# The second image pair with pixel parity alternating by row, and the half-height tap products of both pairs as quarter tiles

## Time and profile before

| | |
|---|---|
| median of 3 runs | 2612.29 us (2609.6 to 2612.97) |
| profiled execution | 2612.23 us, its span 2610.4 us |
| mean granted PE clock | 0.989 |
| instructions | 117000, of them 46070 matmuls |
| DMA | 155.07 MB, mean 59 GB/s |
| input loaded, first block | 0 to 143 us |
| sweeps 0 to 3 | 143 to 1249 us |
| sweeps 4 to 7 | 1261 to 2366 us |
| last block | to 2610 us |

### The profile page before, as it was taken

The page is one execution under the profiler, slowest core; times in us unless marked ns, Lnnn a source line. Parts: engine busy times, 40 slices in busy tenths (PEclk is TensorE's granted clock), DMA queues, the critical chain, the costliest instruction groups (busy, mean ns, idle before and its releaser), DMA issues. The chain is left out here.

```text
span 2610.4 us, 117000 instructions
## 1 busy us (share of the span) xinstructions
PE 2509.8 (96%) x46070; PEld 2417.0 (93%) x46070; DVE 1813.5 (69%) x5782; ACT 1236.6 (47%) x2705; POOL 352.7 (14%) x547
## 2 busy tenths in 40 slices
PE   1999999999999999999899999999999999998998
PEld 1389999999999999999899999999999999997885
DVE  7866666666666666677666666666666666777986
ACT  0866664222233333377666642222333333675877
POOL 1620000000000000066000000000000000653545
PEclk9999999999999999999999999999999999998999
DMA  7810001222450000087600012223600000430006
GB/s 270 219 45 0 0 0 36 61 60 60 91 54 0 0 4 1 0 258 161 190 8 0 0 29 60 60 60 88 66 0 0 0 0 0 129 97 2 4 4 258
DMA packets 323834, 155.07 MB, mean 59 GB/s; under 512 B 155169, under 2 KB 319650, under 8 KB 319650
## 3 DMA queue, kind: packets, MB, share of 16 engines
q1 hardware_dynamic: 321600, 153.41, 22.9%
q10 hardware_dynamic: 2146, 0.53, 0.1%
HBM read 70.00 MB, written 50.33 MB: 46 GB/s over the span
## 5 line engine op out<-in xcount | busy, mean ns | idle before, releaser
L870 PE MATMUL banks<-x_row,w_taps 128*64 128x124 f32 (+2 forms) x40640 | 2200.4, 270 | 5.4 <-DVE x_row L1114 3.1
L870 PEld LDWEIGHTS banks<-x_row,w_taps 128*64 128x64 f32 x40640 | 2198.8, 135 | 7.1 <-issue 6.1
L1123 DVE SCALAR_TENSOR_TENSOR x_row<-banks,sweep_nbias,biased_row 128x128 f32<-128x128 f32 x2032 | 712.9, 351 | 717.1 <-PE banks L870 695.1
L666 ACT ACTIVATE biased_row<-state,sweep_bias 128x256 f32 (+1 forms) x762 | 512.2, 673 | 1038.9 <-DVE state L1126 605.7
L662 ACT ACTIVATE biased_row<-state,aff,gn_a 128x64 f32 (+1 forms) x1016 | 364.2, 429 | 184.4 <-DVE state L1132 184.4
L1126 DVE SCALAR_TENSOR_TENSOR state<-banks,sweep_nbias,biased_row 128x128 f32 (+1 forms) x1016 | 443.0, 436 | 0.0
L550 POOL TENSOR_TENSOR state<-state,stripe_a 128x256 f32<-128x256 f32 x96 | 66.9, 733 | 1982.3 <-DVE state L1126 1962.0
L1132 DVE SCALAR_TENSOR_TENSOR state<-banks,sweep_nbias,biased_row 128x64 f32 (+1 forms) x1016 | 236.9, 275 | 0.1
L1132 DVE SCALAR_TENSOR_TENSOR turn_ring<-banks,sweep_nbias,biased_row 128x64 f32<-128x64 f32 x1016 | 236.7, 274 | 0.0
L843 PE MATMUL banks<-res,ffn_w 64*64 64x512 f32 x512 | 112.3, 597 | 6.1 <-ACT res L599 5.2
L832 PE MATMUL banks<-state,ffn_s 64*64 64x512 f32 x512 | 106.8, 598 | 0.2 <-DVE ffn_s L1285 0.2
(11 more groups left out here) (138 smaller groups left out, 903.3 us busy)
## 6 DMA issues: line engine op xcount, KB each, us to landing
state<-turn_ring SPq DMA_DIRECT2D x512, 64.0 KB, 1.9
resid<-state SPq DMA_DIRECT2D x94, 256.0 KB, 3.6
state<-x_in SPq DMA_DIRECT2D x16, 1024.0 KB, 20.7
stripe_a<-resid SPq DMA_DIRECT2D x32, 512.0 KB, 5.3
stripe_b<-resid SPq DMA_DIRECT2D x32, 512.0 KB, 5.4
out_y<-state SPq DMA_DIRECT2D x16, 1024.0 KB, 4.1
res<-resid SPq DMA_DIRECT2D x32, 256.0 KB, 7.3
resid<-state SPq DMA_DIRECT2D x16, 512.0 KB, 6.7
```

The source lines that it names most:

```text
L666: nc.scalar.activation(as_cells(n, biased_row[:, k, :, :]), cells(n, slice(0, B), i, k, g), ACT.Identity, bias=sweep_bias[:, n:n + 1]).the ...
L870: last = nc.tensor.matmul(out_ps[blk, :, lo:hi], w_taps[:, n % 2, s, blk], x_row[c][src][:, :, s + lo:s + hi], start=at == 0, stop=at == T ...
L1123: nc.vector.scalar_tensor_tensor(x_row[c][par][:, :, 2:2 + HALF], ps, nb, br, ALU.max, ALU.add).then_inc(row_ready[c], 1)
```

## The change

The second image pair gets another layout: pixel parity sits on partition half q in even rows and on the other half in odd rows. In the sweeps down and up its conv therefore reads from the halves crosswise in turn, step by step. The weights are kept as ten 64-column slots (nine taps and one unused) per partition half, in two versions, one with the halves exchanged; the unused slots are never read. A conv now consists of four whole products for each output parity (shifts 2, 1, 3, and shift 0 for one parity with shift 4 for the other) and of the two remaining half-height ones, `single_taps`: 64x64 tiles, the diagonal quarters of the array for pair 0, the others for pair 1. Pair 0 has them at its end and pair 1 at its start, so that the four are neighbours in PE's program, and PE's wait for pair 1's row moves ahead of pair 0's last whole product.

With that go:
- block 0's result is kept as `resid_rows` in DRAM in its own layout, and the odd rows of images 2 and 3 are read back with the halves exchanged (`swap_back`), two chunks behind; `turn_residual` then makes `resid` from it by 64 DMAs inside DRAM, on SyncE's queue before sweep 1's turning; ScalarE waits for the swapped chunks in sweep 0;
- in the turned sweeps only images 0 and 1 go through `turn_ring` and DMAs. The second pair needs no move across partitions; GpSimd stores its rows with two copies a step (`store_turned`), and VectorE writes only `x_row` for it, after `row_stored[1]` of two steps before;
- between the blocks `cross` is four DMAs of half the size in place of two;
- after sweep 7 all odd rows are stored to DRAM and, once the kv products are done, those of images 2 and 3 are read back exchanged, 64 DMAs on SyncE's queue ahead of the output's stores; PE waits for them in the last feed-forward net before image 2 of each chunk, and ScalarE and GpSimd wait for the store;
- `gram_sb` and `o1_a` now lie in the weight buffer; `gram_sb` is zeroed after sweep 6; the memset of `w_taps` goes.

The core of the diff (lines that only declare semaphores, or waits of the same form, left out):

```diff
-        turn_ring = sb("turn_ring", [P, 2, 2, 2, B, WH])
-        w_taps = sb("w_taps", [P, 2, TAPS2, P])
+        turn_ring = sb("turn_ring", [P, 2, 2, 2, 2, WH])
+        w_taps = sb("w_taps", [P, 2, 2, 2 * TAPS2, C])
...
+            def swap_back(j, odd, done):
+                view = resid_rows.rearrange("p (hp r g b w) -> p hp r g b w", r=2, g=2, b=B, w=WH)
+                hp = slice(j * CR // 2, (j + 1) * CR // 2)
+                for q in range(2):
+                    into, frm = slice(q * C, (q + 1) * C), slice((1 - q) * C, (2 - q) * C)
+                    for g in range(2):
+                        sp.dma_start(state_b[into, hp, odd, g, 2:4, :].rearrange("c hp b w -> c hp (b w)"),
+                                     view[frm, hp, odd, g, 2:4, :].rearrange("c hp b w -> c hp (b w)")).then_inc(done, 16)
+            for j in range(CHUNKS + SWAP_LAG):
+                if j < CHUNKS:
+                    sp.wait_ge(ffn_added, j * B + B)
+                    sp.dma_start(resid_rows[:, j * CR * ROW:(j + 1) * CR * ROW],
+                                 state[:, j * CR:(j + 1) * CR, :, :, :].rearrange("p r g b w -> p (r g b w)")).then_inc(rows_kept[j], 16)
+                if j >= SWAP_LAG:
+                    sp.wait_ge(rows_kept[j - SWAP_LAG], 16)
...
+                    swap_back(j - SWAP_LAG, 1, rows_swapped[j - SWAP_LAG])
...
+                for q in range(2):
                     for r in range(2):
+                        block(slice(0, 2), q, r, r, q)
+                        block(slice(2, 4), q, r, q ^ r, q)
+            for part in range(TURN_PARTS):
+                turn_residual(slice(part * PAIRS // TURN_PARTS, (part + 1) * PAIRS // TURN_PARTS))
...
+            sp.wait_ge(last_rows_kept, 32)
+            sp.wait_ge(kv_done, KV_TILES)
+            for j in range(CHUNKS):
+                swap_back(j, 1, rows_swapped[j])
...
+                def store(i, k):
+                    pool.wait_ge(row_ready[1], i * 2 + (hbase(n) + k))
+                    row = x_row[1][slot(n, k)]
+                    for blk, at in ((low, row_of(True, i, k)), (high, row_of(True, i, 1 - k))):
+                        if k == 0 and blk == high:
+                            pool.wait_ge(biased_row_ready, i * 2 + (row_count(n) + 1))
+                        last = nc.gpsimd.tensor_copy(state[blk, at, :, 2:4, :],
+                                                     by_halves(row[blk, :, 2:2 + HALF]))
+                    last.then_inc(row_stored[1], 1)
...
-                pe.wait_ge(row_ready[c], hcount)
-                for at, s in enumerate(TAP_ORDER):
-                    lo, hi = max(0, EDGE - s), min(HALF, HALF + EDGE - s)
-                    for q in range(2):
-                        blk = slice(q * C, (q + 1) * C)
-                        last = nc.tensor.matmul(out_ps[blk, :, lo:hi], w_taps[:, n % 2, s, blk], x_row[c][src][:, :, s + lo:s + hi],
-                                                start=at == 0, stop=at == TAPS2 - 1)
+                halves_of = [slice(q * C, (q + 1) * C) for q in range(2)]
+                weights = w_taps[:, n % 2, 1 if c and not par else 0]
+                crossed = c and par
+                def product(inner, r, s, start, stop):
+                    lo, hi = (0, HALF) if start else (max(0, EDGE - s), min(HALF, HALF + EDGE - s))
+                    return nc.tensor.matmul(out_ps[halves_of[1 - r if crossed else r], :, lo:hi], weights[inner, 2 * s + 1 - r, :],
+                                            x_row[c][src][inner, :, s + lo:s + hi], start=start, stop=stop)
+                def whole_taps(starting):
+                    for at in range(TAPS2 - 1):
+                        for r in range(2):
+                            if c == 0 and r and at == TAPS2 - 2:
+                                pe.wait_ge(row_ready[1], hcount)
+                            last = product(slice(0, P), r, TAP_ORDER[at] if at < TAPS2 - 2 else (0, TAPS2 - 1)[r],
+                                           starting and at == 0, not starting and at == TAPS2 - 2)
+                    return last
+                def single_taps(starting):
+                    for r, s in enumerate((TAPS2 - 1, 0)):
+                        last = product(halves_of[1 - r if c and not par else r], r, s, starting, not starting)
+                    return last
+                if c == 0:
+                    pe.wait_ge(row_ready[0], hcount)
+                    whole_taps(True)
+                    last = single_taps(False)
+                else:
+                    single_taps(True)
+                    last = whole_taps(False)
                 last.then_inc(conv_done[c], 1)
...
+                    if turning and c and not (isinstance(i, int) and i == 0):
+                        dve.wait_ge(row_stored[1], i * 2 + (n0 + k - 2))
                     nc.vector.scalar_tensor_tensor(x_row[c][par][:, :, 2:2 + HALF], ps, nb, br,
                                                    ALU.max, ALU.add).then_inc(row_ready[c], 1)
+                    if turning and c:
+                        return
```

More of the change, by code:

```diff
@@ L183, in build_program @@
         pair_turned = [sem(f"pair_turned{k}") for k in range(2)]
-        resid_stored = sem("resid_stored")
+        rows_kept = [sem(f"rows_kept{j}") for j in range(CHUNKS)]
+        rows_swapped = [sem(f"rows_swapped{j}") for j in range(CHUNKS)]
+        last_rows_kept = sem("last_rows_kept")
+        resid_turned = sem("resid_turned")
         chunk_stored = [sem(f"chunk_stored{j}") for j in range(CHUNKS)]
@@ new lines, in _, with turn_residual, block @@
+            load_taps(1)
+            def turn_residual(hp):
+                def block(images, q, r, to_q, to_s):
+                    old = resid_rows.rearrange("(q c) (hp r g b w) -> q r hp c g b w", q=2, r=2, g=2, b=B, w=WH)
+                    new = resid.rearrange("hp (q c) s (g b w) -> q s hp c g b w", q=2, g=2, b=B)
+                    for g in range(2):
+                        sp.dma_start(new[to_q, to_s, hp, :, g, images, :].rearrange("hp c b w -> hp c (b w)"),
+                                     old[q, r, hp, :, g, images, :].rearrange("hp c b w -> hp c (b w)")).then_inc(resid_turned, 16)
@@ L550, in add_residual, with store_turned @@
                         nc.gpsimd.tensor_tensor(quad_cells(z, b), quad_cells(z, b), quad_residual(z, b), ALU.add).then_inc(resid_added, 1)
+            def store_turned(layer):
+                n = 4 * layer + 1
+                low, high = slice(0, C), slice(C, P)
+                pool.wait_ge(row_stored[1], STEPS * n)
+                pool.wait_ge(biased_row_ready, row_count(n) + 1)
+                pool.wait_ge(basis_ready, 1)
+                pool.wait_ge(first_row_scaled, B * (layer + 1))
+                pool_done(nc.gpsimd.tensor_copy(state[high, H - 2, :, 2:4, :], state[high, H - 1, :, 2:4, :]))
+                def store(i, k):
[7 more added lines that the diff above has]
+                    last.then_inc(row_stored[1], 1)
+                store(0, 1)
+                for i in range(1, PAIRS):
+                    for k in range(2):
+                        store(i, k)
             scale_first_row(0)
             helmert_basis()
+            store_turned(0)
             add_residual(0)
             scale_first_row(1)
+            store_turned(1)
             add_residual(1)
+            pool.wait_ge(conv_done[1], STEPS * 7)
+            nc.gpsimd.memset(gram_sb[:], 0.0).then_inc(gram_zeroed, 1)
             for n in range(KV_TILES):
@@ L713, in rows @@
                 else:
-                    for start, stop in ((2 if n == 0 else 1, WH), (WH, PAIRS)):
+                    for start, stop in ((1, WH), (WH, PAIRS)):
                         with act.Fori(start, stop) as i:
@@ L828, in up @@
                 def up(j, b):
+                    if layer and b == 2:
+                        pe.wait_ge(rows_swapped[j], 128)
                     for q in range(2):
```

88 lines of the change are left out of this document (48 added, 40 removed).

## The result

The changed kernel takes **2761.23 us** (median of four runs, 2756.78 to 2761.29), the kernel before 2612.57 on the same chip: 1.0567 times as long, interval 1.0549 to 1.0586. It is slower, by 149 us, where 191 us less was forecast. The profiled execution took 2756.78 us, its span is 2755.0: 144.6 over the span before. The first rival, the draining switches, is what happened, and above its own 2695 us.

The account below looks back on a forecast made before the run. TensorE, hardly resting and streaming conv columns, was taken to bound the kernel. The terms -210 + 10 + 5 - 2 + 1 + 5 = -191 took 2612 us to 2421 us; range 2398 to 2725.

Parts of the forecast that it names:

- The first rival: Switches before and after the quarters drain TensorE, 0.14 us each, two a step: 2695 us, up to 2817; chance 0.33.
- Going from 128-row tiles to 64-row tiles and back, twice a step: Tile height changes around the quarters in each step: 0 to 0.20 us a switch, taken as 0.
- the streaming of four quarters at once: In the convs, four 64x64 products run together: 1136 columns a step in place of 1256, 210 us less.
- the number of instructions: In the convs of a step, the instruction count was to stay 40.
- The chain around a pair: Pair 1's row is needed half a conv earlier: 1.94 us against 1.959 of streaming, 10 ns a step added, +10 us.
- The turned sweeps: Sweeps 1 and 5: GpSimd's two copies, 0.8 to 1.5 us a step, covered by the conv stream; cost 0.
- Second half of sweeps 3 and 7: Batch statistics every second step make the second pair's result 0.08 us late, x 60: +5 us.
- start: First block, SyncE's stores and read-backs: sweep 0 waits for chunk 0 alone, -2 us.
- the 64 transfers inside DRAM: On SyncE's queue ahead of sweep 1's turning: 145 us, hidden in the 250 of sweep 0.
- the boundary: Between the layers, the first crossing is four DMAs for two, 0.65 us each: +1 us.
- the tail: After the last kv product, 64 read-backs go ahead of the output's stores: +5 us, upper bound +36.

Follow-up runs that it names:

- whole_five: The changed kernel with each pair's two half-height products made full-height again, zeros in the unused weight slots, so no change of tile height; 2656.19 us.
- wait_later: The changed kernel with PE's wait for pair 1's row one product later, just ahead of the quarters; 2727.99 us.
- wait_order: The changed kernel with VectorE's wait for GpSimd's store put ahead of its wait for the conv in the turned sweeps; 2759.4 us.

## Why the prediction was wrong

**The step that failed** is "Going from 128-row tiles to 64-row tiles and back, twice a step": a change of tile height, which I had between 0 and 0.20 us, was taken at 0. It costs 0.150 us put alone into the kernel before, and in the changed kernel (2.281 - 2.178 + 0.214) / 2 = 0.158, where 0.214 are the 124 columns that whole_five has more. Two in 1016 steps are 322 us where the streaming gives back 210. It is a little more than the 0.14 that I had worked out from the earlier trace rows for a switch "of that kind". The records around one switch show the same two parts: the first product of the new shape starts 0.09 us later than in a run (401.102 after 400.904, 0.198 for some 0.105), and its second pass up to 0.05 us later, for a weight load that couldn't go ahead. Both parts were right, 0.09 for the wait and 0.05 for the exposed load as half that of 128 columns; what was wrong was to think that the height could be exempt. My argument was that a 64-row and a 128-row product have the same latency, 156 and 162 ns beyond their streaming. That is true, but it doesn't follow that a product of the one shape may start while the other is under way. The rule cited from the Trainium skill, "TensorEngine Tiling (Array Packing)", Key Properties, holds for the height as well: here the trace of the changed kernel agrees, 0.16 us a change. Why a change costs 8 ns more in the changed kernel than in the kernel before is open; at 0.150 the two would be 305 us.

**Right:** the streaming of four quarters at once (1.95 us of loads against 1.959); the number of instructions.

**The chain around a pair:** 10 ns a step forecast, 11 measured in the plain sweeps (wait_later gives them back). The size is luck in part: I had the chain 0.02 us shorter than the streaming and added 10 ns for what won't line up, and it is 0.011 longer. The same wait one product later costs nothing.

**The turned sweeps** were taken at 0, with GpSimd's copies as the only suspect. The copies take 0.62 us a step, less than the 0.8 to 1.5 estimated, and are covered. The step missed was the other half of the same line of the diff: the added wait sits in front of VectorE's write, and with it the wait for the conv moved to the instruction before. That puts the write 0.112 us after the conv in place of 0.025. 0.085 us x 254 steps = 22 us.

**Second half of sweeps 3 and 7:** +5 us forecast, 0 measured (their step is 2.280 us as elsewhere). The longer step leaves VectorE more time; whether the forecast holds at 1.96 us a step no run shows. The order of time on VectorE, against the earlier trace rows: the write at 2452.99, right behind a statistic, comes 2.28 us after pair 0's last one (2450.71), and pair 1's is in place at 2454.23.

```profile
2452.49 0.41 DVE L1294 BATCH_NORM_STATS2 stats<-state 128x6 f32<-128x256 f32 x1
2452.99 0.35 DVE L1234 SCALAR_TENSOR_TENSOR x_row<-banks,sweep_nbias,biased_row 128x128 f32<-128x128 f32 x1
...
2454.23 0.35 DVE L1234 SCALAR_TENSOR_TENSOR x_row<-banks,sweep_nbias,biased_row 128x128 f32<-128x128 f32 x1 [0.29 <-PE banks L954]
```

**SyncE:** start -2 forecast, -1.5 measured; the 64 transfers inside DRAM took 77 us of issuing, not 145, and were hidden; the boundary +1 forecast, +1.3 measured; the tail +5 forecast, +5.8 measured (7 to 9 in the profiles of the runs that have the same tail). The sweeps end 138.8 us later than before (2505.4 against 2366.6). In the old frame the read-backs are issued from 2528.9 to 2572.5 (forecast 2530 to 2572) and the kernel ends at 2616.2 (forecast 2613 + 3). The boundary's 1.3 us are in the first step of sweep 4, 3.585 us for 2.281: four crossing DMAs take SyncE 2.7 us, and ScalarE waits for them with a row that VectorE and PE need.

```profile
1332.91 2.71 SPq L438 DMA_DIRECT2D state<-resid  x4
1333.63 2.76 ACT L741 ACTIVATE biased_row<-state,aff,gn_a 128x64 f32 x8 [3.06 <-DMA state<-resid]
1335.17 0.35 DVE L1234 SCALAR_TENSOR_TENSOR x_row<-banks,sweep_nbias,biased_row 128x128 f32<-128x128 f32 x1 [2.20 <-ACT biased_row L741]
```

**The sum again,** with the measured terms: -210 + 11 + 322 (switches) + 22 (wait on VectorE) - 1.5 + 1.3 + 5.8 = +151; the profiled execution says +144.6. That the steps close is bookkeeping, since 0.158 was itself taken from them. Of the 6 us between, 1 is the count (from first to last write a sweep has 126 steps, 1008 in all), 1.5 the kernel before's own (its steps in the first halves of five sweeps are 0.002 to 0.010 us above 2.160) and 1 the shorter way from a turned sweep to the next (5.8 and 6.3 us for 6.5 and 6.6); the rest I didn't trace.

**The rival** had the right mechanism and came out at 2695 us with 0.14 a switch, no step slack and no wait on VectorE. With 0.158 (37 us), the slack (11) and the wait (22) it would have been 2765. I had it at 0.33, below the forecast, because all the switches seen changed the width. That was a reason to say that the trace doesn't decide, not a reason to prefer the cheaper end: the switches that the trace did show, all of width, cost 0.19 (0.09 and 0.10 for a load of 128 columns), not the 0.14 that the rival's "every switch seen costs that" puts on them; 0.14 was already the estimate for 64 columns. And a rule named this one as the same kind. The upper end of the range, 2725, was set from the centre of that rival and not from its bound of 2817.

## What to carry to other kernels

A shorter stream is worth its columns only if what surrounds it stays of one shape. Here each change of tile height cost 0.15 to 0.16 us, the streaming of some 90 columns of both passes; count the changes in a step before counting columns. A second wait can cost though it always holds, when it pushes the wait that comes last onto the instruction before: look at which instruction carries the late wait, and put the early one on an instruction of the same engine that nobody waits for. And where the nearest rows all show a price, the zero end of the bounds needs a row of its own to be the forecast.

## What the runs showed of the hardware

- A change between 128x64 and 64x64 tiles, with the same width, cost 0.150 us (2 and 4 a step: +305 and +609 us in 1016 steps) and 0.158 in the changed kernel. It shows as 0.16 to 0.17 us without a weight load, named "issue", while PE counts as busy.
- VectorE's write starts 0.025 us after the semaphore of the conv when it carries that wait itself. With a second, long satisfied wait on the write, the conv's wait sat on the instruction ahead, and the write came 0.112 us after the semaphore (a register instruction ahead, changed kernel) or 0.093 (a semaphore instruction ahead, wait_order). In a link that sets the step this cost 22 us in 254 steps, and moving the second wait off took it back (2761.23 to 2739.07 us).
- A written-out loop on PE stood still 8 of 60 us while the DMA engines were 0.90 busy, and not in 130 us at 0.02. Each stretch of over 0.25 us ended 1.3 to 1.7 us after a 16 KB packet of its instructions had landed.
